# A fused attention and expert block on one core: attention of one half batch issued beside the experts of the half batch before it

## What is computed

```python
x = layernorm(x + attn(x))
x = layernorm(x + moe(x) + shared(x))
# attn: 16 heads of 8 features
q = x @ Wq
lat = (x @ Wk + x @ Wv) @ W_down_kv
k, v = lat @ W_up_k, lat @ W_up_v
s = clip(q_h @ k_h.T * scale)                 # per head, 1024 x 1024
s = clip(s * exp(-1e-4 * abs(i - j)))         # decay by distance
out = softmax(s) @ v_h                        # then @ Wo
# moe: 8 experts, the best 2 of each token, weights by softmax of their 2 logits
h = x @ fc1_w[e]                              # 128 -> 2 x 128
y = (silu(h[:, :128]) * h[:, 128:]) @ fc2_w[e]
# shared: silu(x @ gate_w) * (x @ up_w) @ down_w, 256 wide, computed as experts 8 and 9
```

## Time and profile before

| what | us |
|---|---|
| median of 3 runs (lowest, highest) | 809.12 (803.93, 811.71) |
| the profiled execution, its own time | 815.1 |
| its span, first to last instruction | 813.1 |
| PE busy | 763.2 (94%) |
| ACT busy | 563.2 (69%) |
| DVE busy | 367.1 (45%) |
| POOL busy | 222.7 (27%) |

### The profile page before, as it was taken

How to read it: one execution, slowest core, us unless ns; L and a number is a source line. 1 busy time by engine, 2 the same in 40 slices (tenths; PEclk the granted TensorE clock), 3 DMA queues, 4 the chain that set the end, 5 groups by cost and what they waited for, 6 DMA issues and landing times. The chain is left out here.

```text
span 813.1 us, 14409 instructions
## 1 busy us (share of the span) xinstructions
PE 763.2 (94%) x4889; PEld 344.9 (42%) x4889; DVE 367.1 (45%) x974; ACT 563.2 (69%) x686; POOL 222.7 (27%) x168
## 2 busy tenths in 40 slices
PE   6736999999999999999999999999999999999996
PEld 4422333333333333333333333334666665665664
DVE  1733233232333233333233333333777777777774
ACT  4635799997999999999999999996222222222221
POOL 1619478392000000000000000000534534534533
PEclk9876699997999999999999999999999999999999
DMA  6489939688323324224233242700000000000000
GB/s 178 160 287 233 318 101 323 233 257 276 86 52 85 70 52 101 54 56 99 52 77 77 52 91 64 174 1 15 1 2 25 27 0 26 26 0 26 13 7 20
DMA packets 27797, 77.17 MB, mean 95 GB/s; under 512 B 2496, under 2 KB 18304, under 8 KB 20608
## 3 DMA queue, kind: packets, MB, share of 16 engines
q1 hardware_dynamic: 24320, 51.74, 25.8%
q0 software_dynamic: 3456, 25.17, 8.5%
HBM read 41.24 MB, written 35.65 MB: 95 GB/s over the span
## 5 line engine op out<-in xcount | busy, mean ns | idle before, releaser
L520 ACT ACTIVATE probs<-ps 128x1024 f32<-128x1024 f32 x480 | 446.8, 1063 | 32.4 <-DVE ps L897 21.9
L661 PE MATMUL ps<-probs,Vring 128*32 128x512 f32 x2048 | 282.4, 624 | 0.7 <-ACT probs L525 0.7
L897 DVE TENSOR_TENSOR ps<-ps,cpk 128x256 f32<-128x256 f32 x256 | 109.9, 432 | 321.4 <-PE ps L646 319.2
L646 PE MATMUL ps<-stacks 32*128 32x512 f32 (+3 forms) x1408 | 221.8, 403 | 17.8 <-DMA stacks<-stack_dram 13.1
L646 PEld LDWEIGHTS ps<-stacks 32*128 32x128 f32 x1408 | 115.9, 189 | 266.1 <-ACT probs L520 222.9
L542 ACT ACTIVATE qT<-ps 128x512 f32<-128x512 f32 x80 | 47.8, 597 | 184.9 <-PE ps L628 184.9
L425 POOL TENSOR_TENSOR small<-small 128x4 f32<-128x4 f32 x8 | 8.2, 1020 | 347.2 <-DVE small L862 347.2
L442 POOL TENSOR_TENSOR kT<-kT 128x512 f32<-128x512 f32 x56 | 71.5, 1276 | 56.9 <-DVE kT L1005 56.1
L753 PEld LDWEIGHTS ps<-stage,kT 128*128 128x128 f32 x512 | 65.0, 191 | 41.2 <-issue 27.5
L753 PE MATMUL ps<-stage,kT 128*128 128x128 f32 x512 | 69.6, 279 | 7.6 <-DVE kT L999 7.5
L999 DVE TENSOR_TENSOR kT<-qT,ps 128x512 f32<-128x512 f32 x80 | 54.3, 683 | 48.3 <-ACT qT L542 47.4
(11 more groups left out here) (115 smaller groups left out, 527.7 us busy)
## 6 DMA issues: line engine op xcount, KB each, us to landing
stacks<-stack_dram SPq DMA_DIRECT2D x64, 512.0 KB, 6.4
stack_dram<-stage POOLq DMA_DIRECT2D x24, 1024.0 KB, 10.6
stack_dram<-stage SPq DMA_DIRECT2D x16, 512.0 KB, 6.0
probs<-in_L_attn_x SPq DMA_DIRECT2D x4, 512.0 KB, 4.8
ptmp<-in_L_attn_x SPq DMA_DIRECT2D x8, 256.0 KB, 3.0
out<-qT SPq DMA_DIRECT2D x8, 256.0 KB, 2.4
rows_sb<-in_decay_rows SPq DMA_DIRECT2D x2, 512.0 KB, 6.6
stage<-in_L_ffn_fc_w SPq DMA_DIRECT2D x1, 1024.0 KB, 8.9
```

The lines of the kernel that those rows point to most:

```text
L520: nc.scalar.activation(probs[:, m % 6, :], slot[m % 3], ACT.Exp, scale=SCALE).then_inc(score_slots_free, 1)
L646: last = mm(slot[m % 3][:, h * HALF + lo - q0:h * HALF + hi - q0], sv[rows, u, 1, v, kt * P:(kt + 1) * P], sv[rows, u, 0, v, lo:hi], start ...
L661: last = mm(bank[6][r:r + 32, :], Vring[:, u, kt, h, :], probs[:, (2 * g + qh) % 6, h * HALF:(h + 1) * HALF], start=(kt == 0), stop=(kt == ...
L897: tt(d, d, diag_fix.unsqueeze(1).to_broadcast([P, 2, P]), ALU.mult).then_inc(diag_done, 1)
```

## The change

All stages are rewritten around half batches ("chunks": 512 queries of one sequence, 8 in all).

- A chunk's attention is four quads of four heads, 8 key tiles each: 32 steps. The stacked rows of four heads fill all 128 rows (`keys`, `queries`), and a step has two score tiles, `scores(2m)` for heads 0 and 1 of the quad (row tiles 0 and 1, banks 0 and 1) and `scores(2m+1)` for heads 2 and 3 (row tiles 2 and 3, banks 2 and 3). There are these two slots, where there were three. The key tiles are taken in the order 0, 4, 1, 5, 2, 6, 3, 7, so that every second step crosses the diagonal.
- A step on PE is: `scores` of the next step, twice; `outputs(m)`, the four column tiles, now with 9 columns of V (8 and the ones); then `beside(c, t)`, which issues at fixed steps t the matmuls of chunk c-1's experts (`up`, `down`, `route`, turns) and the projections of chunk c+2. `take(c, t)` is the same table for DVE. The products of `beside` go to three banks in turn (5 to 7); PE waits for DVE to have taken the one three back.
- In steps 10 to 29 one half of an expert's up product stands in every step, and a down product in every second one.
- SiLU is tanh on ACT (the same activation table as the exponential) and two DVE instructions. ACT no longer copies q, k, v, x out of PSUM in the main part: DVE does.
- POOL splits chunk c+2 while chunk c runs, and computes the squares and the powers.
- The preparation ahead of the first score has two chunks (one sequence), not four sequences.
- The fast path runs always, unrolled, without loops. The flag is read near its end, and the general path follows behind `If` and computes everything again where needed (not here).

The core of the diff:

```diff
-                    pe.wait_ge(score_slots_free, i * TPB + (m + 1))
-                    q0, q1 = qh * HALF, (qh + 1) * HALF
...
-                def group_step(i, g, tiles_left=True):
-                    if tiles_left or 2 * g + 4 < TILES:
-                        score_tile(i, 2 * g + 4)
...
-                    output_group(i, g)
-                    if tiles_left or 2 * g + 5 < TILES:
-                        score_tile(i, 2 * g + 5)
+                if n >= 2:
+                    pe.wait_ge(exp_done, n - 1)
+                cut = min(max(kt * P - c % 2 * HALF, 0), HALF)
+                for v, lo, hi in ((1, 0, cut), (0, cut, HALF)):
+                    if lo == hi:
+                        continue
+                    for i in (2 * j, 2 * j + 1):
+                        rows = slice(i * HROWS, (i + 1) * HROWS)
+                        last = mm(bank[i][:, lo:hi], keys[rows, u, kt // CT, v, tok(kt % CT)], queries[rows, u, v, lo:hi],
+                                  start=True, stop=True)
+                last.then_inc(scores_ready, 1)
...
+            for c in range(NCH + 1):
+                for t in range(TPC):
+                    m = c * TPC + t
+                    if m + 1 < TILES:
+                        scores(2 * m + 2)
+                        scores(2 * m + 3)
+                    if m < TILES:
+                        outputs(m)
+                    beside(c, t)
...
+                if t == 7 and has_p:
+                    keep(("k", p), qk[:, p % 2, 1, :])
+                if t == 7 and has_d:
+                    ln1_rows(d)
+                if t == 7 and has_p:
+                    keep_values(p, taken(("v", p))).then_inc(side_kept, 1)
...
+                if p < NCH:
+                    pool.wait_ge(side_kept, numbers["k", p])
+                    squares_of(p)
+                    split(0, p, 1)
+                    split_end()
+                    split(1, p, 0)
+                    split(1, p, 1)
+                    split_end()
```

More of the change, by code:

```diff
@@ new lines, in step @@
+            def step(c, t):
+                d, m = c - 1, c * TPC + t
+                if d >= 0 and t >= 11 and t % 2 == 1 and t <= 11 + 2 * (NE - 1):
+                    tanh_part(d, (t - 11) // 2)
+                if m + 1 < TILES:
+                    exponential(2 * m + 2)
+                    exponential(2 * m + 3)
+            exponential(0)
+            exponential(1)
+            for c in range(NCH + 1):
+                for t in range(TPC):
+                    step(c, t)
+            act.wait_ge(side_kept, numbers["flag", 0])
@@ new lines, in down @@
+            def down(d, e):
+                dst = side(("dn", d, e))
+                pe.wait_ge(side_kept, numbers["g", d, min(e, E) if e < E else NE - 1])
+                for t in range(CT):
+                    last = mm(dst[:, tok(t)], hid[:, e % 3, tok(t)], dn_sb[:, e, :], start=True, stop=(e < E))
+                    if e == E:
+                        last = mm(dst[:, tok(t)], hid[:, (e + 1) % 3, tok(t)], dn_sb[:, e + 1, :], start=False, stop=True)
+                last.then_inc(side_ready, 1)
@@ L852, in _, with taken @@
[L852 to L854 removed]
+            link(copy(head_sum_h[:, :], head_sum))
+            dve.wait_ge(s_rows, 32)
+            dve.wait_ge(first_kept, 4)
+            split(0, 0)
+            dve.wait_ge(first_kept, 5)
+            split(1, 1)
+            for h in range(2):
+                dve.wait_ge(first_ready, 5 + h)
+                keep_values(h, bank[6 + h]).then_inc(first_v_kept, 1)
+            count = [0]
+            def taken(name):
+                count[0] += 1
+                assert numbers[name] == count[0], name
+                dve.wait_ge(side_ready, count[0])
+                return side_bank(name)
@@ new lines, in _ @@
+            fix_diagonal(0)
+            fix_diagonal(1)
+            for c in range(NCH + 2):
+                for t in range(TPC if c <= NCH else 4):
+                    m = c * TPC + t
+                    if m + 1 < TILES:
+                        fix_diagonal(2 * m + 2)
+                        fix_diagonal(2 * m + 3)
+                    take(c, t)
+                    if m < TILES and t % NT == NT - 1:
+                        evacuate(m // NT)
+            assert count[0] == len(numbers)
```

1550 lines of the change are left out of this document (819 added, 731 removed).

## The result

882.93 us median of 4 runs (881.64 to 884.51), against 809.18 us for the kernel before on the same chip: ratio 1.0922, 95% interval 1.0864 to 1.0979. The kernel became 9.2% slower. The profiled execution has a span of 879.6 us.

The account below looks back on a forecast made before the run. PE was taken as full in attention and experts. Head 59, chunks 725.5, tail 52 and 2 around gave 838.5; 5 x (7 + 6) = 65 for pile-up and clock made 903.5, scaled 0.7% down to 897 us (870 to 925; 8 in 10: 805 to 960).

Parts of the forecast that it names:

- Overlapping gives nothing since PE is full in both stages: Attention and experts: PE full in both, so a chunk costs 95 or 91 us against 89 before, with preparation in it.
- Score tile 0.42 for both when four row tiles run at once: Each attention step on PE: both score tiles issued together take 0.42 us; 0.84 kept as the other bound.
- Round trip 4.48 + B with the diagonal, 3.95 + B without: Two successive steps, score to exponential to output: at least these us, B being PE's work beside attention.
- Head, first scores at 56, and 3 for the half clock: Before chunk 0: first scores at 56 us, not 64.3, plus some 3 for half clock after idling: 59.
- Tail 52: After the last attention, chunk 7's experts alone: 12 us chain, 26 products, 3 half clock, 11 to the end.
- Pile-up in step 7 or 8: DVE's rows behind POOL's instructions: Chunks 1 to 5: POOL holds up DVE's layernorm rows, 3.9 us alternating or 9 by gaps; PE idles 5 to 10, taken 7.
- The clock behind it, 6 us per chunk: Chunks 1 to 5, after PE's step 8 wait: some 15 us at half clock, losing 6 us each.
- chunks of over 105 us: Sign that the forecast is right: chunks lasting over 105 us.
- 95 and 91 us for odd and even chunks without the pile-up: Chunk lengths: steps 10 to 29 take 63 us odd, 58 plus 1.5 even; the other 12 steps 31.4.
- No pile-up: Rival, chance 0.22: in step 7 the layernorm rows slip through before POOL starts, or POOL is late; 832 us, up to 845.
- PE packed: Rival, chance 0.15: round trip not felt, score tiles always together, DVE never late; 734 us, up to 795 with some waits.
- Worse still: Rival, chance 0.13: four row tiles don't run at once, or the clock falls also in chunk 0; 940 to 960 us.

Follow-up runs that it names:

- the filled wait: Kernel after, plus five products of 512 columns on PE during its wait in step 8 of chunks 1 to 5: 878.56 us, ratio 1.0888.
- The first edit: Kernel after, with POOL's squares and splits starting only after DVE's four layernorm rows: 865.6 us, ratio 1.0751.
- tiles-apart kernel: Kernel after, with PE issuing the first score tile, the output group, then the second score tile, instead of both score tiles first: 1062.34 us, ratio 1.3174.
- kernel with both edits: Kernel after, with POOL's squares and splits after DVE's layernorm rows and the diagonal-crossing head pair second in each step: 831.65 us, ratio 1.0301.

## Why the prediction was right

897 us were forecast, 882.93 measured, and the mechanism is the one forecast. In terms of the profiled execution the sum was 903.5 against a span of 879.6 and 2 around it: 22 us too much. By its steps:

- *Overlapping gives nothing since PE is full in both stages.* Right: PE's busy time moved by 5 us only.
- *Score tile 0.42 for both when four row tiles run at once.* Right: 0.44 and 0.49 from both tiles' start to the output group's. By the rate that the Trainium skill ("TensorE: Matmul & The Clock Gate", measured speedup vs the span model) states, the prediction had an estimate of 0.55; the trace stays below that.
- *Round trip 4.48 + B with the diagonal, 3.95 + B without.* Right. Two steps of chunk 0 take 4.46 (forecast 4.48), the chunk 76.9 (77); a pair of expert steps in odd chunks 6.41 (6.33), and leaving the correction out gave 42 us (36 to 41 expected).
- *Head, first scores at 56, and 3 for the half clock.* The first scores began at 50.81, 5.2 before the 56, and the first exponential, behind their correction, at 52.10, 7 before the 59. The first store was placed right (issued at 23.05, forecast 24), but the 12 took 16.19 us and not 12 x 1.73 = 20.8, and from the issue of the first quad's loads at 44.62 to the scores it was 6.2 us and not 9 to 10. The half clock behind it lies inside chunk 0, whose 76.9 hold it.
- *Tail 52.* It took 58.4. The chain from the last output to the router's product ran from 821.2 to 840.0, 18.8 us where 12 were taken. The granted clock of the tail, 0.81, is 2 x 0.19 x 58.4 = 22 us at half speed, much of it in that chain. This term was mis-sized.
- *Pile-up in step 7 or 8: DVE's rows behind POOL's instructions.* Right in place and kind. Of the two ends given, 3.9 by turns and 9 by gaps, the rows alternate: 4.50 - 1.11 = 3.4 us more. PE waits 4.43, the forecast took 7 and named 5 or more as the sign of it.
- *The clock behind it, 6 us per chunk.* Wrong in size: stretches of 6.8 us, not 15, and 1.5 us each by the filled wait. The 15 was read from one place in the kernel before, where PE waited and POOL and the loads went on. So pile-up and clock together were put at 13 per chunk. From the trace they are about 4.4 + 1.5 = 6. The first edit, which took away 3.4 of the wait and 27 of the 37 us at half clock, gave 21.7 in chunks 1 to 5, 4.3 each. So the sign "chunks of over 105 us" didn't come true either: they took 98.3 to 103.2.
- *95 and 91 us for odd and even chunks without the pile-up.* Too low by 2 to 3 for the odd and by 1 to 2 for the even: without pile-up and clock, 103.2 - 6 = 97 and 98.3 - 6 = 92; chunk 7 took 96.6 for 93.5, chunk 6 89.8 for 88. Steps 10 to 29 took 63.9 in odd chunks (63 forecast) and 60.8 in even ones (58, and 1.5 for turns, route and norms). So in odd chunks most of it lies in the other 12 steps, in even ones it lies in the expert steps; no run takes it further.

Pile-up and clock (-35 in all) and the head with its 3 us (-7) were oversized, the chunks (+14) and the tail (+6) undersized: -22. The forecast came out closer than its largest error, which is luck. Luck too is that the medians differ by 14 and not by 22: the sum was taken down by 0.7%, since the kernel before ran that much slower in its profiled execution than in its median, while the kernel after ran 0.15% faster in its own (881.64). *No pile-up* is excluded by the trace, and where the first edit took most of it away the time was 866, not 832 to 845. *PE packed* needs steps of 1.86 in chunk 0; they take 2.23 with nothing beside (84.53 to 88.99) and 2.4 on average. *Worse still*: row tiles are concurrent and chunk 0 kept its clock, at 0.96; in the tiles-apart kernel the same chunk fell to 0.60.

## What to carry to other kernels

Look first whether the engine that bounds both stages is the same one: then overlapping them can save only that engine's idle time, here 50 us, unless its work itself gets shorter, and new waits in the mixed loop can cost more than that. With fewer PSUM slots (no run here has a third one, so what the slot alone is worth isn't shown), write down the round trip (score to exponential to output) next to the bounding engine's work for two successive steps; what lies in it, like a correction ahead of the exponential, costs up to its full length, and putting an uncorrected tile first gave back 33 us without removing an instruction. And order a burst on POOL behind DVE's short SBUF to SBUF rows, not beside them, when PE waits behind these rows.

## What was not expected of the hardware

A DVE row from SBUF to SBUF of 128x128 takes 0.34 us alone and 1.05 to 1.30 beside POOL instructions of 1.0 and 1.3: one row per POOL instruction. The Trainium skill ("SBUF — State Buffer", Terms) says that DVE and POOL share a pair of ports of which one holds the whole pair for its instruction and the other is blocked. The trace agrees that DVE is held for a whole instruction, and adds the order for these rows: the two take turns, so that the run of POOL instructions delays DVE by one of them per row, not by its whole length. That is no general rule. The copy of rows 7 began at 75.99 inside this POOL instruction of the kernel before and ended at 79.81, behind the whole next one:

```profile
75.02 2.39 POOL L378 TENSOR_TENSOR ptmp<-kT,rows_sb 128x1024 f32<-128x1024 f32 x1
```

What decides between the two isn't shown. The four matmuls of four row tiles, 512 columns each, lie inside 0.55 us; those of two lay inside 0.50.

The clock reacts to more than long waits. In the kernel after, a wait of 4.43 us is followed by 6.8 us at half clock, but so is, for 3.4 us, a wait of 1.04 after smaller ones (the first edit, chunk 3). The same waits in its chunks 1 and 5 (1.05), and waits of 1.34 in the kernel with both edits, are not, so the length of a wait alone doesn't tell. In the kernel after, chunk 0, where PE is busy 65.8 of 76.9 us, is at 0.96. With the score tiles apart the same chunk stays at half clock for most of 121 us with PE busy 90.4. A loop can thus run far slower than its sum of waits says. What decides between these cases isn't settled here.
